# Two graph layers on one core: output shifts, the second group's point at infinity, the first group's distances and masks, the first load's semaphore and the tail's norms in other places of the order

## The chip, the core and the metric

The kernel runs on one core of a Trainium2 chip. The metric is the device time of one execution in microseconds (us); the median of three runs is given. One execution was also recorded by the hardware profiler.

## What is computed

32 graphs of 256 nodes with 128 features pass through two layers with a residual and a layer norm after each:

```python
s = x @ w_se.T + b_se                       # three coordinates per node
A = jnp.exp(-dist(s)) * adj                 # distances, masked
x_nmp = A @ relu(x @ w_msg.T + b_msg)
x_conv = relu(bn2(conv17(relu(bn1(conv1(x))))) + x)
g = gru(input=[x_conv, x_nmp], state=x)     # gates r, z, n
y = layernorm(x + g)
h = (1 + eps) * y + adj @ y
out = layernorm(y + relu(h @ W1 + b1) @ W2 + b2)
```

## The kernel before

Features lie on the 128 partitions. The 32 graphs are worked in eight groups of four (GB = 4), each group as two pairs of graphs with 512 columns (h = 0 and 1). The program is a pipeline written out by hand: each engine has its own list of calls, `prologue`, `steady(s, u, front)` for s = 1 to 7 (s = 3 to 6 in a hardware loop) and `last`. In `steady(s)` the group gb = s - 1 goes through its gates, first norm, aggregation over `adjT`, the two-layer perceptron (`mlp1`, `hidden`, `mlp2`) and second norm, the group gm = s through its messages, distances and convolution, and gf = s + 1 is begun. Nothing but the order of the calls and the semaphore waits in them sets the order of the work.

The 17-tap convolution is worked by interpolation: seven points (HALF, ZERO, PLUS2, MINUS2, PLUS1, MINUS1, INF) have 4 or 5 taps each. A point has a stream of data (`sv`) and a set of weights (`traw`). In groups 0 (all of them), 1 (HALF, ZERO, PLUS2) and 2 (HALF, PLUS2) `plain_taps` multiplies them in float32. Elsewhere `taps` needs each in a high and a low part: ACT makes the high ones (`stream_high` into `sth`, `tap_high` into `wh`), DVE the low ones (`stream_low` into `stl`, `tap_low` into `wl`), and three products stand for one. `W_ORDER` says in which order the weights' parts are made; `w_count(n)` is the count of the semaphores w_high and w_low at which n is ready. The raw weights of ZERO and INF lie in the buffer `tail`, which `hidden` (ACT) and `add_b2` (POOL) write from s = 1 on. The matrices `x`, `nmp`, `xconv` and `h` are split in the same way (`x_low`, `nmp_low`, `xconv_low`, `h_low` on DVE).

What the change touches:

- Start. SP issues `first`, the first pair of x, a part of conv2 and the second pair of x, waits until that pair is there (X_LOADED), and only then issues group 1's x, the identity, the perceptron's weights, group 0's adjacency and the gates' weights. ACT issues three other parts of conv2 and the message weights.
- First group. PE makes the convolution's points with `distances` (four graphs) and `nmp` in between. ACT makes the exponentials (`exps`), POOL masks graphs 0 and 1 (`first_mask`), DVE graphs 2 and 3 (`mask`). DVE adds the points up in `u_sum`, `pair2_sum`, `pair1_sum`, `pair2_add`, `pair1_add`, `inf_add`, and makes group 1's streams (`first_diffs`, `half_stream`, `zero_stream`, `parts2`); POOL's `streams2(1)` follows `parts2(1)`.
- Second group (s = 1, `second_group` on DVE). PE's `taps(1, INF)` wait for `tap_low(INF)` and `stream_low(1, 4)`; behind them stand `mlp1`, `mlp2(0, 0)` and `conv1(2, .)`, and the latter wait for `x_low(2, .)`.
- Every `steady` with front (s = 1 to 6). DVE ends with `nmp_low`, `xconv_low` and `out_shift` of both pairs. `out_shift` (128x4) needs the second norm's 1/deviation from POOL. ACT's `out_norm` (eight activations of 128x128) waits for it; behind `out_norm` ACT has the next stage's `msg_out` and `gates`. PE's fourth gate product (`inn`) uses the bank of the first and so waits for ACT's tanh of it (TR_READY).
- Tail (`last`, group 7). Its second pair is halved: items (0, WHOLE), (1, 0), (1, 1). ACT normalizes the output of the first two, DVE that of the third, each stored by SP in this order.

Of the kernel before, what the change touches and what calls it, by code (L numbers as in the profile page):

```python
# [96 lines left out]
def gnn_kernel(nc, t, out):  # L97
# [10 lines left out]
    with ctx:  # L108
# [99 lines left out]
        W_ORDER = ("conv1", "gates", PLUS1, MINUS2, MINUS1, ZERO, INF, "w1", HALF, PLUS2)  # L208
# [15 lines left out]
        X_LOADED = stage("x_loaded", 16)  # L224
# [84 lines left out]
        x_pair0_loaded = sem("x_pair0_loaded")  # L309
        conv2_loaded = sem("conv2_loaded")  # L310
# [54 lines left out]
        def halved(c):  # L365
            return c in (0, 1)
# [101 lines left out]
        def _(sp):  # L468
# [6 lines left out]
            def store(g, h, c=None):  # L475
                if (h, c) == LAST_ITEMS[-1]:
                    wait(sp, LAST_READY, g, 1)
                else:
                    wait(sp, OT_READY, g, item(h, c) + 1)
# [4 lines left out]
            def prologue():  # L484
# [3 lines left out]
                done(sp.dma_start(xv[0][:, cols(1)], x_v[0, :, cols(1)]), X_LOADED)  # L488
                wait(sp, X_LOADED, 0, 16)
# [34 lines left out]
        def _(pool):  # L524
# [66 lines left out]
            def prologue():  # L591
# [12 lines left out]
                streams2(0)  # L604
                first_mask(0)
# [54 lines left out]
        def _(act):  # L660
# [102 lines left out]
            def prologue():  # L763
# [12 lines left out]
                wait(act, X_LOADED, 0, 16)  # L776
# [26 lines left out]
                tap_high(ZERO)  # L803
# [3 lines left out]
                tap_high(INF)  # L807
                act.wait_ge(mlp_loaded, 16)
                act.activation(w1h[:, :], w1raw, ACT.Copy).then_inc(w_high, 1)
                tap_high(HALF)  # L810
                tap_high(PLUS2)

            def steady(s, u, front):
# [21 lines left out]
                exps(gm, 3)  # L835
                hidden(gb, 0)
# [21 lines left out]
            def last(g, u):  # L858
# [8 lines left out]
                for h, c in LAST_ITEMS[:-1]:  # L867
                    out_norm(g, h, c)
# [5 lines left out]
        def _(dve):  # L874
# [214 lines left out]
            def y_apply(g, h, c=None):  # L1089
                src, v = y_block(h, c), place(h, c)  # L1090
                wait(dve, RSTD[0], g, item(h, c) + 1)
                for q in part_blocks(c):
                    last = dve.tensor_scalar(xn[:, h, q, :], src(q, q + 1), stats[:, 0, v, q, 1:2], rstd[:, 0, v, q:q + 1],  # L1093
                                             ALU.subtract, ALU.mult)
                done(last, XN_READY)
# [43 lines left out]
            def prologue():  # L1139
# [68 lines left out]
                pair2_sum(0)  # L1208
                first_stream1(MINUS1, ALU.subtract)
                taps_step(minus1, minus1, -1.0, even)  # L1210
                mask(0, 0, 3)
                dve.wait_ge(tap_sums, steps[0])
# [3 lines left out]
                parts2(1)  # L1216
                pair1_sum(0)
# [13 lines left out]
            def second_group():  # L1231
# [22 lines left out]
                tap_low(ZERO)  # L1254
                y_apply(0, 1)
                mask(1, 1, 0)
                mask(1, 1, 1)
                inf_stream(1)
                tap_low(INF)
# [3 lines left out]
                h_low(0, 1)  # L1263
                mask(1, 1, 2)
# [4 lines left out]
            def steady(s, u, front):  # L1269
# [40 lines left out]
                if front:  # L1310
# [22 lines left out]
            def last(g, u):  # L1333
# [5 lines left out]
                gates(g, u, 1, 1)  # L1339
# [23 lines left out]
        def _(pe):  # L1363
# [227 lines left out]
            def prologue():  # L1591
# [14 lines left out]
                for b in range(GB):  # L1606
                    distances(0, b)
# [103 lines left out]
```

## Time and profile before

| | us |
|---|---|
| median of 3 runs | 377.34 (377.03 to 377.43) |
| the profiled execution | 380.05 |
| its span (first to last instruction) | 378.2 |
| PE busy | 364.7 (96%) |
| DVE busy | 322.8 (85%) |
| ACT busy | 230.0 (61%) |
| POOL busy | 154.1 (41%) |

PE is the matrix engine (PEld its weight loads), DVE the vector engine, ACT the scalar engine, POOL GpSimd, SP the engine that issues most transfers. In the profile "busy" of PE has modelled ends, so two matmuls that follow at once overlap in it. A number in square brackets is the idle time of the engine before the row, with what released it. L876 is line 876 of the kernel before.

### The profile page before, as it was taken

Reading aid. Unit: us, or ns where it says so; the run is one execution under the profiler, and the core shown is the slowest. Engines: PE = TensorE matmul, PEld = TensorE weight load, DVE = VectorE, ACT = ScalarE, POOL = GpSimd, SP = SyncE. Lnnn points to the kernel's source line nnn. Section 1 sums busy time; section 2 is a strip of 40 time slices with the busy share of each in tenths; the row PEclk is TensorE's granted clock in tenths of the full one; section 3 lists DMA queues with packets and bytes.
Section 4 is the critical chain, followed back from the end, with each engine's and each line's share of the span. In section 5 each row is a group of like instructions: output and inputs, shape, how many; then the busy total and the mean of one; then the engine's idle time right before and its main releaser. Section 6 shows DMA issues by size and latency. Waiting matters only on the chain.

```text
span 378.2 us, 6430 instructions
## 1 busy us (share of the span) xinstructions
PE 364.7 (96%) x2150; PEld 317.2 (84%) x2150; DVE 322.8 (85%) x706; ACT 230.0 (61%) x436; POOL 154.1 (41%) x158
## 2 busy tenths in 40 slices
PE   6999999899899999999999999999999999999994
PEld 4778889698698988899888997989888997988973
DVE  3999999989799988989799897998889897995584
ACT  3455765444867467573866648774676639564765
POOL 3112326136242743528323462517425372234362
PEclk9899999899999999999999999999999999999999
DMA  6700004300113010120112001120101301000002
GB/s 196 270 1 2 0 3 166 113 1 2 55 56 113 1 57 1 55 113 3 55 55 75 39 10 46 55 111 0 55 0 55 111 2 55 2 0 2 0 30 83
DMA packets 8135, 19.39 MB, mean 51 GB/s; under 512 B 688, under 2 KB 5168, under 8 KB 7088
## 3 DMA queue, kind: packets, MB, share of 16 engines
q1 hardware_dynamic: 7536, 18.17, 13.9%
q10 hardware_dynamic: 576, 0.92, 0.7%
q8 instruction: 13, 0.21, 0.2%
q14 instruction: 10, 0.08, 0.1%
HBM read 14.90 MB, written 4.19 MB: 50 GB/s over the span
## 4 chain that ended last, share of the span: by engine, by line
PE 73%; DVE 13%; ACT 6%; POOL 3%; issue 2%; DMA 2%; SPq 0%; ACTq 0%; DVEq 0%
PE back L1368 24%; PE conv L1368 20%; PE back L1482 6%; PE front L1482 5%; PE back L1578 5%; PE conv L1421 3%; PE front L1454 2%; ACT tail L749 2%; PE front L1474 2%; DMA xv<-in_x_dram 2%; PE back L1534 2%; DVE xcl L1036 1%; DVE xn L1093 1%; ACT tail L756 1%; DVE stl L876 1%
## 5 line engine op out<-in xcount | busy, mean ns | idle before, releaser
L1368 PE MATMUL conv<-sth,wh 128*128 128x256 f32 x207 | 62.2, 301 | 1.7 <-DVE wl L1133 1.7
L1368 PE MATMUL conv<-sth,wl 128*128 128x256 f32 x207 | 59.2, 286 | 0.0
L1368 PE MATMUL conv<-stl,wh 128*128 128x256 f32 x207 | 59.1, 286 | 0.0
L552 POOL TENSOR_TENSOR rstd<-rstd,small 128x4 f32<-128x4 f32 (+1 forms) x34 | 38.5, 1134 | 44.5 <-DVE rstd L1075 43.9
L1368 PEld LDWEIGHTS conv<-sth,wh 128*128 128x128 f32 x207 | 39.2, 189 | 3.0 <-DVE wl L1133 1.8
L1368 PEld LDWEIGHTS conv<-stl,wh 128*128 128x128 f32 x207 | 39.3, 190 | 0.2
L1368 PEld LDWEIGHTS conv<-sth,wl 128*128 128x128 f32 x207 | 39.4, 190 | 0.0
L662 ACT ACTIVATE sth<-sv 128x272 fp32r<-128x272 f32 (+1 forms) x33 | 17.3, 524 | 34.4 <-DVE sv L904 18.5
L557 POOL TENSOR_TENSOR xw<-xw,xv 128x512 f32<-128x512 f32 (+1 forms) x15 | 18.5, 1234 | 46.9 <-ACT xw L732 46.9
L749 ACT ACTIVATE tail<-tail,shift,rstd 128x128 f32<-128x128 f32 x60 | 24.1, 482 | 20.6 <-DVE shift L1128 20.6
L589 POOL TENSOR_TENSOR adjT<-adjT,diag 128x256 f32<-128x256 f32 x32 | 27.9, 902 | 7.0 <-DVE msg L950 3.6
L528 POOL TENSOR_TENSOR av<-h 128x544 f32<-128x544 f32 x6 | 8.6, 1436 | 54.0 <-ACT h L677 54.0
L1482 PE MATMUL front<-amat,msg 128*128 128x256 f32 x128 | 29.1, 379 | 0.0
L1482 PE MATMUL back<-adjT,xn 128*128 128x256 f32 x120 | 28.2, 387 | 0.8 <-DVE xn L1093 0.8
L1578 PEld LDWEIGHTS back<-later_w,tail 128*128 128x128 f32 x224 | 26.3, 192 | 0.7
L756 ACT ACTIVATE tail<-back,first_w 128x512 f32<-128x512 f32 (+1 forms) x30 | 20.4, 683 | 10.3 <-PE back L1368 10.3
L1578 PE MATMUL back<-later_w,tail 128*128 128x128 f32 x224 | 26.5, 275 | 0.0
L1482 PEld LDWEIGHTS front<-amat,msg 128*128 128x128 f32 x128 | 23.8, 190 | 2.9
L1482 PEld LDWEIGHTS back<-adjT,xn 128*128 128x128 f32 x120 | 21.9, 189 | 5.2 <-DVE xn L1093 1.4
L1093 DVE TENSOR_SCALAR xn<-back,stats,rstd 128x128 f32<-128x128 f32 x60 | 20.5, 404 | 2.8 <-POOL rstd L552 2.1
L1050 DVE SCALAR_TENSOR_TENSOR gbuf<-gbuf 128x512 f32<-128x512 f32 (+1 forms) x17 | 13.6, 800 | 9.1 <-ACT gbuf L723 9.1
L876 DVE TENSOR_TENSOR stl<-sv,sth 128x272 fp32r<-128x272 f32 (+1 forms) x33 | 18.4, 557 | 3.0 <-ACT sth L662 2.9
(243 smaller groups left out, 1029.2 us busy)
## 6 DMA issues: line engine op xcount, KB each, us to landing
adjT<-in_adj_dram SPq DMA_DIRECT2D x8, 1024.0 KB, 4.8
out_dram<-tail SPq DMA_DIRECT2D x15, 256.0 KB, 2.2
xv<-in_x_dram SPq DMA_DIRECT2D x7, 512.0 KB, 3.3
tail<-in_conv_dram ACTq DMA_DIRECT2D x3, 256.0 KB, 4.6
gbuf<-in_gates_dram SPq DMA_DIRECT2D x1, 576.0 KB, 8.6
xv<-in_x_dram SPq DMA_DIRECT2D x2, 256.0 KB, 5.5
tail<-in_conv_dram SPq DMA_DIRECT2D x1, 320.0 KB, 5.3
later_w<-in_later_dram SPq DMA_DIRECT2D x1, 320.0 KB, 5.7
```

The source lines that it names most:

```text
L552: done(pool.tensor_tensor(rstd[:, k, v, q], rstd[:, k, v, q], minus_half[:, q], ALU.pow), RSTD[k])
L557: done(pool.tensor_tensor(xw[:, h, part(c)], xw[:, h, part(c)], xv[u][:, part_cols(h, c)], ALU.mult), XWX_READY)
L589: done(pool.tensor_tensor(dg, dg, diag[:, :].unsqueeze(1).to_broadcast([P, PAR, P]), ALU.add), ADJE_READY)
L662: done(act.activation(dst, src, ACT.Copy), name)
L749: last = act.activation(o[:, q, :], o[:, q, :], ACT.Identity, bias=shift[:, v, q:q + 1], scale=rstd[:, 1, v, q:q + 1])
L756: done(act.activation(hid[:, h, f, part(c)], bank("hid", h, c, f), ACT.Relu, bias=vec[:, B1 + f:B1 + f + 1]), HID_READY)
L876: done(dve.tensor_tensor(dst, src, full(hi), ALU.subtract), name)
L1050: done(dve.scalar_tensor_tensor(ghn[:, h, part(c)], tr[:, h, part(c)], 1.0, ghn[:, h, part(c)], ALU.add, ALU.mult), T1_READY)
L1093: last = dve.tensor_scalar(xn[:, h, q, :], src(q, q + 1), stats[:, 0, v, q, 1:2], rstd[:, 0, v, q:q + 1], ALU.subtract, ALU.mult)
L1368: ins = pe.matmul(bank, a, b, start=first and k == 0, stop=last and k == len(todo) - 1)
L1482: ins = pe.matmul(tile[:, k * N:(k + 1) * N], lhs(b, rm), rhs(b, rm), start=rm == 0, stop=rm == PAR - 1)
L1578: ins = pe.matmul(tile[:, k * P:(k + 1) * P], hid[:, h, f, q * P:(q + 1) * P], w2[:, f, :], start=f == 0, stop=f == 1)
```

## The change

Calls change places; few waits come or go, and the arithmetic is the same.

- SP issues its first transfers without the wait. The second pair of x has a semaphore of its own, x_pair1_loaded, and X_LOADED counts from group 1.
- First group: PE's distances stand between the taps of MINUS2. DVE's `mask(0, 0, 3)` and `pair2_sum(0)` come behind `parts2(1)`. POOL's masks wait for the weight sum of PLUS1 (tap_sums 10).
- Second group: INF's weights are split before ZERO's, `inf_stream(1)` stands ahead of the masks, `tap_low(ZERO)` behind `h_low(0, 1)`. `hidden` on ACT waits for ZERO's low weights in s = 1. POOL's `add_b2` had that wait and keeps it, but its count is now 8 in place of 6.
- Stages with front: `out_shift(gb, 0)` stands ahead of `nmp_low`, `out_shift(gb, 1)` ahead of `xconv_low`.
- Tail: DVE's first norm of pair 0 is cut in two around `add_input(1, 1)`; PE's aggregation of pair 0 is in one piece behind the last transposes; the output norm of item (1, 0) goes from ACT (two activations and a shift) to DVE (two `tensor_scalar`).

`plain_taps` gets a range of taps, `y_apply` a list of blocks; PE's waits in `plain_conv1` and `messages` follow the new semaphores. The core of the diff:

```diff
-        W_ORDER = ("conv1", "gates", PLUS1, MINUS2, MINUS1, ZERO, INF, "w1", HALF, PLUS2)
+        W_ORDER = ("conv1", "gates", PLUS1, MINUS2, MINUS1, INF, "w1", ZERO, HALF, PLUS2)
...
-        X_LOADED = stage("x_loaded", 16)
+        X_LOADED = stage("x_loaded", 16, 1)
...
             def store(g, h, c=None):
-                if (h, c) == LAST_ITEMS[-1]:
-                    wait(sp, LAST_READY, g, 1)
+                if halved(c):
+                    wait(sp, LAST_READY, g, item(h, c))
...
-                done(sp.dma_start(xv[0][:, cols(1)], x_v[0, :, cols(1)]), X_LOADED)
-                wait(sp, X_LOADED, 0, 16)
+                sp.dma_start(xv[0][:, cols(1)], x_v[0, :, cols(1)]).then_inc(x_pair1_loaded, 16)
                 load_x(1, 1)
...
                 streams2(0)
+                pool.wait_ge(tap_sums, 10)
                 first_mask(0)
...
                 xconv_high(0, 0)
-                tap_high(ZERO)
+                tap_high(INF)
                 nmp_high(0, 1)
                 xconv_high(0, 1)
                 stream_high(1, 2)
-                tap_high(INF)
                 act.wait_ge(mlp_loaded, 16)
                 act.activation(w1h[:, :], w1raw, ACT.Copy).then_inc(w_high, 1)
+                tap_high(ZERO)
...
                 exps(gm, 3)
+                if first:
+                    act.wait_ge(w_low, w_count(ZERO))
                 hidden(gb, 0)
...
-                for h, c in LAST_ITEMS[:-1]:
-                    out_norm(g, h, c)
+                out_norm(g, 0, WHOLE)
...
                 mask(0, 0, 2)
-                pair2_sum(0)
                 first_stream1(MINUS1, ALU.subtract)
                 taps_step(minus1, minus1, -1.0, even)
-                mask(0, 0, 3)
-                dve.wait_ge(tap_sums, steps[0])
                 first_diffs(1)
                 half_stream(1)
                 zero_stream(1)
                 parts2(1)
+                dve.wait_ge(tap_sums, steps[0])
+                mask(0, 0, 3)
+                pair2_sum(0)
                 pair1_sum(0)
...
                 pair2_sum(1)
-                tap_low(ZERO)
+                tap_low(INF)
                 y_apply(0, 1)
+                inf_stream(1)
                 mask(1, 1, 0)
                 mask(1, 1, 1)
-                inf_stream(1)
-                tap_low(INF)
                 stream_low(1, 4)
                 h_low(0, 0)
                 w_low_part(w1l[:, :], w1raw, w1h[:, :], w_count("w1"))
                 h_low(0, 1)
+                tap_low(ZERO)
...
                     stream_low(gf, 2)
+                    out_shift(gb, 0)
                     nmp_low(gm, 0)
                     nmp_low(gm, 1)
+                    out_shift(gb, 1)
                     xconv_low(gm, 0)
                     xconv_low(gm, 1)
-                    out_shift(gb, 0)
-                    out_shift(gb, 1)
...
-                gates(g, u, 1, 1)
-                y_apply(g, 0, WHOLE)
+                reset(g, 1, 1)
+                y_apply(g, 0, WHOLE, (0, 1))
+                add_input(g, 1, 1)
+                y_apply(g, 0, WHOLE, (2, 3))
                 gates_end(g, 1, 1)
...
                 out_stats(g, 1, 1)
-                out_shift(g, 1, 0)
+                out_apply(g, 1, 0)
                 out_apply(g, 1, 1)
...
-                plain_taps(0, MINUS2)
-                for b in range(GB):
-                    distances(0, b)
+                plain_taps(0, MINUS2, 0, 3)
+                distances(0, 0)
+                distances(0, 1)
+                plain_taps(0, MINUS2, 3)
+                distances(0, 2)
+                distances(0, 3)
                 plain_taps(0, PLUS1)
...
                 mlp2(g - 1, 1)
-                aggregate(g, u, 0, WHOLE, (0,))
                 y_transpose(g, 1, 1)
-                aggregate(g, u, 0, WHOLE, (1,))
+                aggregate(g, u, 0, WHOLE)
```

How DVE's order moves in the first group, between `mask(0, 0, 2)` and `pair2_add`; the first sv is MINUS1's stream, amat a mask, av to wv are group 1's streams, pm the sums of point pairs. Before:

```order
L1005 SCALAR_TENSOR_TENSOR pm<-conv,first_w,pm 128x4x64 [waits conv_minus2_ready]
L1005 SCALAR_TENSOR_TENSOR pm<-conv,first_w,pm 128x4x64
L898 TENSOR_TENSOR sv<-vv 128x272 [waits pair1_parts_ready]
L1177 SCALAR_TENSOR_TENSOR adjT<-adjT 128x640 [waits tap_sums]
L982 TENSOR_TENSOR amat<-front,adjT 128x512 [waits adj_loaded,exp_ready]
L891 TENSOR_TENSOR av<-h 128x4x2x68 [waits inf_stream_ready,h1_ready,tap_sums]
L893 TENSOR_TENSOR av<-h 128x4x2x68
L904 SCALAR_TENSOR_TENSOR sv<-av 128x544 [waits sub0_full,token_diffs_ready]
L912 SCALAR_TENSOR_TENSOR sv<-sv 128x272 [waits sub1_full,half_stream_ready]
L917 SCALAR_TENSOR_TENSOR wv<-av 128x272 [waits pair2_streams_ready]
L919 SCALAR_TENSOR_TENSOR wv<-av 128x272
L1018 SCALAR_TENSOR_TENSOR pm<-conv,first_w,pm 128x512 [waits conv_minus1_ready]
```

With the change:

```order
L900 TENSOR_TENSOR sv<-vv 128x272 [waits pair1_parts_ready]
L1180 SCALAR_TENSOR_TENSOR adjT<-adjT 128x640 [waits tap_sums]
L893 TENSOR_TENSOR av<-h 128x4x2x68 [waits inf_stream_ready,h1_ready]
L895 TENSOR_TENSOR av<-h 128x4x2x68
L906 SCALAR_TENSOR_TENSOR sv<-av 128x544 [waits sub0_full,token_diffs_ready]
L914 SCALAR_TENSOR_TENSOR sv<-sv 128x272 [waits sub1_full,half_stream_ready]
L919 SCALAR_TENSOR_TENSOR wv<-av 128x272 [waits pair2_streams_ready]
L921 SCALAR_TENSOR_TENSOR wv<-av 128x272
L984 TENSOR_TENSOR amat<-front,adjT 128x512 [waits adj_loaded,exp_ready,tap_sums]
L1007 SCALAR_TENSOR_TENSOR pm<-conv,first_w,pm 128x4x64 [waits conv_minus2_ready]
L1007 SCALAR_TENSOR_TENSOR pm<-conv,first_w,pm 128x4x64
L1020 SCALAR_TENSOR_TENSOR pm<-conv,first_w,pm 128x512 [waits conv_minus1_ready]
```

The mask of graph 3 and the two `pair2_sum` operations moved behind group 1's streams, next to `pair1_sum`.

DVE in the second group, behind the first norm of pair 1. wl<-tail is a `tap_low`, sv the stream at infinity, stl its low part, nmpl<-back an `h_low`. Before:

```order
L982 TENSOR_TENSOR amat<-front,adjT 128x512 [waits nmp_full,adj_loaded,exp_ready] x2
L938 SCALAR_TENSOR_TENSOR sv<-av 128x4x67 [waits inf_stream_ready]
L942 SCALAR_TENSOR_TENSOR sv<-sv 128x272 [waits sub6_full,inf_part_ready]
L1133 TENSOR_TENSOR wl<-tail,wh 128x512 [waits w_high]
L876 TENSOR_TENSOR stl<-sv,sth 128x272 [waits streams_high_ready]
L876 TENSOR_TENSOR nmpl<-back,nmph 128x512 [waits h_high_ready]
L1133 TENSOR_TENSOR w1l<-later_w,w1h 128x256 [waits w_high]
L876 TENSOR_TENSOR nmpl<-back,nmph 128x512 [waits h_high_ready]
```

With the change:

```order
L940 SCALAR_TENSOR_TENSOR sv<-av 128x4x67 [waits inf_stream_ready]
L944 SCALAR_TENSOR_TENSOR sv<-sv 128x272 [waits sub6_full,inf_part_ready]
L984 TENSOR_TENSOR amat<-front,adjT 128x512 [waits nmp_full,adj_loaded,exp_ready] x2
L878 TENSOR_TENSOR stl<-sv,sth 128x272 [waits streams_high_ready]
L878 TENSOR_TENSOR nmpl<-back,nmph 128x512 [waits h_high_ready]
L1136 TENSOR_TENSOR w1l<-later_w,w1h 128x256 [waits w_high]
L878 TENSOR_TENSOR nmpl<-back,nmph 128x512 [waits h_high_ready]
L1136 TENSOR_TENSOR wl<-tail,wh 128x512 [waits w_high]
```

The stream at infinity moved ahead of the masks, and the `tap_low` that stands here is now ZERO's and comes last.

DVE at the end of a stage with front (s = 1 here; the same in all six). Before:

```order
L876 TENSOR_TENSOR stl<-sv,sth 128x544 [waits streams_high_ready]
L876 TENSOR_TENSOR nmpl<-front,nmph 128x512 [waits nmp_high_ready] x2
L1036 SCALAR_TENSOR_TENSOR xcl<-usum,xch 128x4x128 [waits xconv_high_ready] x2
L1128 SCALAR_TENSOR_TENSOR shift<-stats,rstd 128x4 [waits rstd2_ready] x2
```

With the change:

```order
L878 TENSOR_TENSOR stl<-sv,sth 128x544 [waits streams_high_ready]
L1131 SCALAR_TENSOR_TENSOR shift<-stats,rstd 128x4 [waits rstd2_ready]
L878 TENSOR_TENSOR nmpl<-front,nmph 128x512 [waits nmp_high_ready] x2
L1131 SCALAR_TENSOR_TENSOR shift<-stats,rstd 128x4 [waits rstd2_ready]
L1038 SCALAR_TENSOR_TENSOR xcl<-usum,xch 128x4x128 [waits xconv_high_ready] x2
```

Each shift moved ahead: one before the two `nmp_low`, one before the two `xconv_low`.

## Rows read from the trace of the kernel before

**Rows 1.** Busy time by windows, 60 to 70 us: PE, PEld, DVE, ACT, POOL, granted clock, DMA.
```profile
60.00:70.00 10.00, 8.34 (x54) 6.84 (x53) 9.90 (x22) 4.45 (x10) 6.67 (x6) 1.00 0.31 115
```
**Rows 2.** Timeline of PE, rows with idle time: start, length, engine, line, operation, [idle, releaser].
```profile
69.60 0.36 PE L1368 MATMUL conv<-sth,wh 128*128 128x256 f32 x1 [1.66 <-DVE wl L1133]
97.54 0.50 PE L1368 MATMUL back<-nmph,wh 128*128 128x512 f32 x1 [1.07 <-ACT gbuf L723]
141.93 0.51 PE L1368 MATMUL back<-nmph,wh 128*128 128x512 f32 x1 [0.25 <-ACT gbuf L723]
363.90 1.97 PE L1482 MATMUL back<-adjT,xn 128*128 128x256 f32 x8 [0.76 <-DVE xn L1093]
```
**Rows 3.** The start: PE's row, the second x pair's landing (L488), a window's traffic.
```profile
8.78 1.86 PE L1438 MATMUL conv<-xv,first_w 128*128 128x512 f32 x2 [1.99 <-DMA xv<-in_x_dram]
...
DMA to landing us min/median/max: 6.6/6.6/6.6
...
5.00:6.00 1.00, 1.00 (x4) 0.49 (x3) 0.72 (x6) 0.42 (x1) 0.00 (x0) 1.00 0.95 350
```
**Rows 4.** Timeline of the first group, and one DVE addition of the second.
```profile
26.64 0.99 PE L1474 MATMUL front<-factT 32*128 32x256 f32 x4 [0.68 <-ACT amat L707]
34.98 0.75 DVE L1018 SCALAR_TENSOR_TENSOR pm<-conv,first_w,pm 128x512 f32<-128x512 f32 x1 [0.16 <-ACT pm L697]
35.63 0.76 POOL L538 TENSOR_TENSOR sv<-wv 128x272 f32<-128x272 f32 x1
35.65 1.29 DVE L1013 TENSOR_TENSOR usum<-usum,pm 128x512 f32<-128x512 f32 x1
...
76.08 0.68 DVE L1013 TENSOR_TENSOR usum<-usum,pm 128x512 f32<-128x512 f32 x1
```
**Rows 5.** Timeline of the second group, 65 to 78 us, POOL, DVE and PE.
```profile
65.27 2.50 POOL L567 TENSOR_TENSOR tail<-xn,later_w 128x512 f32<-128x512 f32 x2
66.57 1.49 DVE L938 SCALAR_TENSOR_TENSOR sv<-av 128x268 f32<-128x268 f32 x1
68.10 0.44 DVE L942 SCALAR_TENSOR_TENSOR sv<-sv 128x272 f32<-128x272 f32 x1
74.88 1.28 DVE L876 TENSOR_TENSOR xl<-xv,xh 128x512 fp32r<-128x512 f32 x2
77.12 0.48 PE L1368 MATMUL conv<-xh,wh 128*128 128x512 f32 x1
```
**Rows 6.** The chain that ended last: the same twelve matmuls of `mlp1`, second group and later.
```profile
71.83 3.76 PE back L1368 x12
...
250.34 2.76 PE back L1368 x12
```
**Rows 7.** End of stage 1, timeline and all shifts' durations (ns min/median/max).
```profile
88.30 1.28 DVE L876 TENSOR_TENSOR nmpl<-front,nmph 128x512 fp32r<-128x512 f32 x2
89.63 1.51 PE L1454 MATMUL front<-later_w,xv 128*128 128x132 f32 x12
92.00 3.20 ACT L749 ACTIVATE tail<-tail,shift,rstd 128x128 f32<-128x128 f32 x8 [3.38 <-DVE shift L1128]
...
L1128 DVE SCALAR_TENSOR_TENSOR shift<-stats,rstd x16: 149/164/692, 91.3 to 374.0; 128x4 f32<-128x4 f32 x15, 128x2 f32<-128x2 f32 x1
```
**Rows 8.** The chain that ended last: a pair's 27 gate matmuls, pair 0 and pair 1.
```profile
180.91 6.44 PE back L1368 x27
187.79 6.25 PE back L1368 x27
```
**Rows 9.** Timeline of the tail: ACT's tanh, DVE's product after it, the last stores.
```profile
359.76 0.49 ACT L735 ACTIVATE gbuf<-gbuf,small 128x256 f32<-128x256 f32 x1
360.77 0.41 DVE L1061 TENSOR_TENSOR gbuf<-gbuf 128x256 f32<-128x256 f32 x1
374.68 0.86 ACT L749 ACTIVATE msg<-msg,shift,rstd 128x128 f32<-128x128 f32 x2
375.57 0.84 SPq L482 DMA_DIRECT2D out_dram<-msg  x2
```

More of the change, by code:

```diff
@@ L309, in gnn_kernel @@
         x_pair0_loaded = sem("x_pair0_loaded")
+        x_pair1_loaded = sem("x_pair1_loaded")
         conv2_loaded = sem("conv2_loaded")
@@ L775, in prologue @@
                 h1_out(0, 1)
-                wait(act, X_LOADED, 0, 16)
+                act.wait_ge(x_pair1_loaded, 16)
                 high(xh[0][:, cols(1)], xv[0][:, cols(1)], XH_READY)
@@ L1087, in y_stats, with y_apply @@
                 norm_stats(0, g, h, c, y_block(h, c))
-            def y_apply(g, h, c=None):
+            def y_apply(g, h, c=None, qs=None):
                 src, v = y_block(h, c), place(h, c)
                 wait(dve, RSTD[0], g, item(h, c) + 1)
-                for q in part_blocks(c):
+                for q in part_blocks(c) if qs is None else qs:
                     last = dve.tensor_scalar(xn[:, h, q, :], src(q, q + 1), stats[:, 0, v, q, 1:2], rstd[:, 0, v, q:q + 1],
                                              ALU.subtract, ALU.mult)
-                done(last, XN_READY)
+                if q == part_blocks(c)[-1]:
+                    done(last, XN_READY)
             def h_low(g, h, c=None):
@@ L1394, in taps, with plain_taps @@
                     done(ins, CONV_FULL[n])
-            def plain_taps(g, n):
-                if n == ZERO:
+            def plain_taps(g, n, k0=0, k1=None):
+                k1 = NTAP[n] if k1 is None else k1
+                if k0 > 0:
+                    pass
+                elif n == ZERO:
                     wait(pe, Z_READY, g, 1)
@@ L1418, in plain_taps @@
                 out = inf_out(g) if n == INF else conv_out(n)
-                for k in range(NTAP[n]):
+                for k in range(k0, k1):
                     at = k + 1 if n == ZERO else k
@@ L1422, in plain_taps @@
                                     stop=k == NTAP[n] - 1)
-                done(ins, CONV_FULL[n])
+                if k1 == NTAP[n]:
+                    done(ins, CONV_FULL[n])
             def conv1(g, u, h, ahead=False):
@@ L1435, in plain_conv1 @@
                     pe.wait_ge(x_pair0_loaded, 16)
+                elif g == 0:
+                    pe.wait_ge(x_pair1_loaded, 16)
                 else:
@@ L1440, in messages @@
             def messages(g, u):
-                if isinstance(g, int) and g < 2:
+                if opening(g):
+                    pe.wait_ge(x_pair0_loaded, 16)
+                    pe.wait_ge(x_pair1_loaded, 16)
+                elif isinstance(g, int) and g == 1:
                     wait(pe, X_LOADED, g, 16)
```

## The prediction, made before the changed kernel was run

> **What bounds the kernel now.** I read the busy times by windows first, then PE's timeline for rows with idle time, then the chain that ended last, and around each idle row the timeline of the engine that it names. The reader should see three regimes.
>
> In the first 75 us DVE has no free time: 9.90 of the 10 us from 60 to 70, while PE has 8.34 [rows 1]. What DVE does there is the path, and whatever shortens it moves everything behind it. Between stages PE waits for ACT once per stage: 1.07 us at 97.54, 0.25 us at 141.93 [rows 2]. In the loop no idle time is shown any more, but the 27 gate matmuls of pair 0 take 6.44 us and those of pair 1 take 6.25 us [rows 8]: 0.19 us of waiting and restarting hide in it. In the tail the chain alternates between engines, with 0.76 us of PE waiting for DVE [rows 2], and ends with two stores one behind the other [rows 9]. The largest single idle time of PE is 1.66 us, up to 69.60, for INF's low weights [rows 2]. It costs more than itself: the same twelve matmuls take 3.76 us from 71.83, right after it, and 2.76 us at 250.34 [rows 6].
>
> **The change part by part.** The sum is made against the profiled execution, 380.05 us with a span of 378.2. The median of the runs is 377.34, and I take the difference over unchanged.
>
> *First transfers.* SP no longer waits before it issues group 1's x and what follows. Nothing on the path waits for any of these, so I take no gain. The loss is bounded by what they may take from the transfers before them, since PE idles for the second x pair until 8.78 and the whole start hangs on it [rows 3]. Between zero (a queue serves in order) and an equal share for group 1's x, 0.5 MB at the 350 GB/s of the window [rows 3], that is 1.5 us. I take zero: ahead of the second pair SP already has three transfers queued without a wait, and it landed 6.6 us after its issue [rows 3], which is what 1.8 MB at about that rate (5.2 us) and a landing need. The Trainium skill ("DMA: Bandwidth & Descriptors", section on queues, rings and completion order) says that a completion's semaphore write lands only after every earlier write of that DMA engine, across its queues. By that rule ACT's last conv2 part and message weights could be reported late, behind writes of group 1's x; no row here shows it, and the sum would stay the same unless conv2's delay exceeded that of the x pair.
>
> *First group.* Two paths meet at `pair1_sum`: DVE waits only 0.16 us there for ACT's output of MINUS1, which waits for PE [rows 4]. Both must be relieved for a gain. PE: with two taps of MINUS2 between the distances, the 0.68 us that PE waited for an exponential [rows 4] is filled. DVE: its work up to `pair1_sum` is the same, but `parts2(1)` is done earlier, by a mask and two sums that now follow it, over 1 us of work. So POOL's `streams2(1)`, whose last operation ran from 35.63 to 36.39, is over before DVE's first addition of two SBUF tensors. That addition started at 35.65 and took 1.29 us; the same one without POOL at work takes 0.68 [rows 4]. The gain is 0.61 + 0.16 = 0.77, at least 0 and at most that; I take 0.75, since mask and sums read PSUM and the longer addition is the one operation in this stretch that shows POOL's neighbourhood. POOL's new wait for tap_sums 10 is satisfied when its first exponential is there or soon after (POOL had been idle before), and PE's `nmp` behind it has the 0.68 us in hand.
>
> *Second group.* DVE's work from the masks to `x_low(2, 0)` is only permuted, but POOL's `add_b2` (two, 2.50 us from 65.27) now waits for ZERO's low weights and leaves the stream at infinity alone: 1.49 us beside it against 0.44 for the next one, of the same size [rows 5]. So `x_low(2, 0)` starts at 74.88 - 1.05 = 73.83 and its first half ends some 0.66 later, at 74.5; PE's `conv1(2, 0)` may start at 74.55 in place of 77.12 [rows 5]. On PE the path up to it is free of the 1.66 and of the slow 1.00 [rows 2, 6]: 77.12 - 2.66 = 74.46. The two meet within 0.1 us; the later one decides, **2.57 us**. Behind this stand ACT's h1, POOL's differences and the next stage, all waiting for `conv1(2, .)`, so it carries on. What could be late next: ACT's `hidden` waits for ZERO's low weights, which DVE makes before the last two masks, some 4 us before `x_low`; `h_low(0, 0)` needs ACT, which was idle up to the stream's high part. `add_b2` is wanted only after `mlp2` and may lie anywhere in the 3 us after. The bounds are 1.05 (DVE's alone, if PE finds another wait) and 2.66.
>
> *Shifts, six stages.* `out_norm` starts 3.38 us before the place it has now at the most [rows 7], and the stall it causes is 1.07 + 0.19, 0.25 + 0.19, and 0.19 in each of the four stages behind: 1.26 + 0.44 + 0.76 = 2.46 us [rows 2, 8]. All fit into 3.38. After that ACT waits for `msg_out` on DVE, whose place does not move. The price is on DVE: two shifts ahead of what PE waits for. A shift alone takes 0.16, beside POOL up to 0.69 [rows 7], and POOL adds the diagonals at just this place. In stage 1 the first `nmp_low` ends at about 88.95 and PE's `messages` take it at 89.63 [rows 7]: 0.68 us of cover against 0.69. I subtract 0.1; in later stages three products per tap stand for one ahead of `messages`, and the cover is longer. That is **2.35 us**, with bounds of 0 (the tanh stays as late, held by DVE's messages) and 2.5. The Trainium skill ("SBUF — State Buffer", on the shared port pair) says that DVE with two SBUF inputs and POOL exclude each other for a whole instruction. The trace agrees, with 0.69 against 0.16; by that rule each of the two shifts could wait for one diagonal operation, and the sum would be the same up to the 0.1 already taken.
>
> *Tail.* The product behind ACT's last tanh could start at 360.25 and started at 360.77, behind four blocks of norm [rows 9]; with two of them ahead it starts 0.5 earlier, and the chain up to `aggregate(1, 0)`, where PE idles 0.76 [rows 2], takes 0.48 of that. PE's aggregation of pair 0 ends later, but before that point. At the end ACT's norm of item (1, 0) ended at 375.54 and its store came at 375.57, the last one 0.42 behind it [rows 9]. On DVE it is ready 0.9 earlier, and the last store then goes when item (1, 1) is ready, some 0.35 sooner. Together 0.83, bounds 0.3 and 0.9.
>
> **Sum:** 0.75 + 2.57 + 2.35 + 0.83 = 6.5 us. Profiled 380.05 - 6.5 = 373.55; median 377.34 - 6.5 = **370.8 us**.
>
> **Rivals.**
> - *Transfers crowd the start.* For: the wait removed is one that keeps 2.5 MB away from the x pair. Against: see above. 1.5 us of the gain go, 372.3.
> - *The second group finds another wait*, such as ACT's `h_high` or `hidden` behind ZERO's weights, so that PE stands still as before. For: DVE is full, and ACT's order has a new wait. Against: each input is ready 0.3 us or more before it is needed by the sums above. Only DVE's 1.05 stays, 372.4.
> - *The shifts give nothing*: ACT's tanh is then bound by `messages` on DVE, which the shifts beside POOL push back. 377.34 - 4.15 = 373.2.
> - *Slower than before.* One mechanism: the queue shares its rate among all it holds, so that the second x pair lands behind all five transfers now queued after it, 2.5 MB. At 350 GB/s that is 7.1 us, at the rate that the second pair's own landing shows (1.8 MB in 6.6 us) [rows 3] 9.2 us; with the latter 377.34 - 6.5 + 9.2 = 380.0. It decides from a landing 6.5 us later. Against: such a share would also have spread the three transfers that already stand together.
> - *It does not do what it says* (the norms and shifts are not earlier because they wait for POOL): in the third rival.
>
> **How the numbers follow.** Forecast 0.70, with its own range 369.9 to 371.8 (all terms near their upper bounds; half a microsecond to one lost). Transfers 0.10, second group 0.09, shifts 0.07, share among all 0.03 (of it 0.01 so near the limit that it reads as no change), the first two rivals together 0.01 (373.9). The range from 369.6 to 372.7 takes in the first three cases and leaves out about 0.11. A measurement can tell about 0.2% (0.75 us) from no change. Faster 0.97, same 0.01, slower 0.02.
>
> **What would show it.** In the changed kernel's profile PE should have no idle row of over 0.6 us between 10 and 360 us; INF's first product should follow the distances at once, with the granted clock at 1.00 from 65 to 75 us; DVE's addition in `pair2_add` of group 0 should take 0.68; pair 0's gates should take 6.25 us in the loop, and its inner stage period should fall by 0.2. The last two stores should be issued 0.4 apart with the last right behind DVE. The second x pair should still start PE at about 8.8. I am wrong if PE starts there later, if `conv1(2, 0)` comes later than about 73.8 (74.55 less the first group's 0.75), or if PE waits for the low parts of `nmp` or `xconv` at a stage's beginning.

## The result, and the profile after

The changed kernel took 372.89 us (median of 6 executions, 372.3 to 374.02), the kernel before, run beside it, 377.38 us (377.03 to 378.57). The ratio is 0.9883 (0.9861 to 0.9904): 4.5 us faster, where 6.5 were forecast, and 0.2 us above the range. The profiled executions tell another size: 380.05 us before and 373.07 us after, 6.98 us apart. Nearly every step that I read from the profile holds when profile is compared with profile. What failed lies between the profile and the median.

PE's timeline of the changed kernel (start, length, engine, line, operation, count, in brackets the idle time before the row and what ended it), its rows with idle time, and last the row that had 0.76 us of it in the tail:

```profile
8.97 1.12 PE L1449 MATMUL conv<-xv,first_w 128*128 128x512 f32 x2 [1.66 <-DMA xv<-in_x_dram]
19.50 2.41 PE L1429 MATMUL conv<-sv,first_w 128*128 128x256 f32 x10 [0.20 <-DVE first_w L1180]
26.07 2.41 PE L1429 MATMUL conv<-sv,gbuf 128*128 128x256 f32 x10 [0.32 <-DVE gbuf L1180]
28.75 1.97 PE L1496 MATMUL front<-amat,msg 128*128 128x256 f32 x8 [0.28 <-DVE amat L984]
73.11 0.47 PE L1373 MATMUL conv<-xh,wh 128*128 128x512 f32 x1 [0.26 <-DVE xl L878]
...
354.95 0.41 PE L1548 MATMUL front<-ident_w,gbuf 128*128 128x128 f32 x2 [0.27 <-DVE gbuf L1066]
...
356.99 1.97 PE L1496 MATMUL back<-adjT,xn 128*128 128x256 f32 x8
```

Of the four idle times in [rows 2], 1.66, 1.07, 0.25 and 0.76 us, none is left. In the first group 0.32 and 0.28 us have come in place of the 0.68 of [rows 4], and 0.27 us is new in the tail. New is also 0.26 us ahead of `conv1(2, 0)`: PE now waits there for DVE's `x_low(2, 0)`. The row of 8.97 answers to the first of [rows 3]: the same two matmuls take 1.12 us where they took 1.86.

DVE's and POOL's timeline of the changed kernel, first group and then second (as [rows 4, 5]):

```profile
33.70 0.77 POOL L538 TENSOR_TENSOR sv<-wv 128x272 f32<-128x272 f32 x1
...
34.86 0.68 DVE L1015 TENSOR_TENSOR usum<-usum,pm 128x512 f32<-128x512 f32 x1
...
63.96 0.43 DVE L940 SCALAR_TENSOR_TENSOR sv<-av 128x268 f32<-128x268 f32 x1
...
72.27 1.29 DVE L878 TENSOR_TENSOR xl<-xv,xh 128x512 fp32r<-128x512 f32 x2
...
68.62 2.57 POOL L567 TENSOR_TENSOR tail<-xn,later_w 128x512 f32<-128x512 f32 x2 [4.73 <-DVE wl L1136]
```

POOL's last operation of `streams2(1)` is over at 34.47, before the addition, which takes 0.68 us in place of 1.29. DVE's step of the INF tile takes 0.43 us in place of 1.49, with POOL's `add_b2` 4.7 us behind it.

The chain that ended last, changed kernel (start, length, engine, tile, line, count), answers to [rows 6, 8]:

```profile
94.48 6.25 PE back L1373 x27
...
113.26 2.76 PE back L1373 x12
...
305.95 6.25 PE back L1373 x27
...
312.64 6.25 PE back L1373 x27
```

Pair 0's gates take 6.25 us like pair 1's. The row at 312.64 stood at 319.07 before, so 6.43 us have been gained by then, and the tail adds 0.57 to make 7.0 us of span.

One row more divides the 6.43: the second group's distances, the last PE row ahead of its aggregation, before and after.

```profile
63.18 0.50 PE L1474 MATMUL front<-factT 32*128 32x256 f32 x4
...
61.76 0.50 PE L1488 MATMUL front<-factT 32*128 32x256 f32 x4
```

Up to there 1.42 us are gained, where the sum has 0.75. From there to `conv1(2, 0)` (77.12 to 73.11, 4.01 in all) it is 2.59, where the sum has 2.57, and from there to the row at 312.64 another 2.42, where it has 2.35. The first figure is too large because the profile before holds a stretch of half clock at 9 us that the sum left out, as the next section shows.

### The profile page after: what moved, and what is told of

The parts are those of the page before. It is cut to its first block, busy times and chain, and to the rows that moved or that the text cites. A ratio compares the mean times of both kernels' runs of the same rounds, so it can differ in the third digit from the quotient of the medians.

```text
span 371.2 us, 6429 instructions
## 1 busy us (share of the span) xinstructions
PE 361.3 (97%) x2150; PEld 315.3 (85%) x2150; DVE 319.2 (86%) x707; ACT 232.2 (63%) x434; POOL 153.6 (41%) x158
## 4 chain that ended last, share of the span: by engine, by line
PE 83%; DVE 11%; DMA 2%; issue 1%; ACT 1%; POOL 0%; SPq 0%; POOLq 0%; DVEq 0%
PE back L1373 28%; PE conv L1373 22%; PE front L1496 8%; PE back L1496 6%; PE back L1592 6%; PE conv L1429 3%; PE front L1468 3%; DMA xv<-in_x_dram 2%; PE back L1548 2%; PE front L1488 1%; DVE adjT L1180 1%; PE conv L1468 1%; DVE amat L984 1%; DVE usum L997 1%; DVE xn L1095 1%
## 5 line engine op out<-in xcount | busy, mean ns | idle before, releaser
L589 POOL TENSOR_TENSOR adjT<-adjT,diag 128x256 f32<-128x256 f32 x32 | 25.1, 813 | 7.5 <-DVE usum L1033 3.9
L729 ACT ACTIVATE gbuf<-back,small 128x512 f32<-128x512 f32 x15 | 10.3, 690 | 20.4 <-PE back L1373 20.4
L567 POOL TENSOR_TENSOR tail<-xn,later_w 128x512 f32<-128x512 f32 x15 | 19.9, 1328 | 7.0 <-DVE wl L1136 4.7
```

Of the source, the lines that this page charges most:

```text
L567: done(pool.tensor_tensor(out_tile(h, c)[:, q, :], xn[:, h, q, :], b2bc.unsqueeze(1).to_broadcast([P, len(part_blocks(c)), D]), ALU.add), ...
L589: done(pool.tensor_tensor(dg, dg, diag[:, :].unsqueeze(1).to_broadcast([P, PAR, P]), ALU.add), ADJE_READY)
```

## Where the profile and the median part

The windows of 9 to 12.5 and 70 to 73.5 us (stretch and length, busy time and count of PE, PEld, DVE, ACT and POOL, granted clock, DMA share, GB/s), first the kernel before, then the changed one:

```profile
9.00:12.50 3.50, 3.50 (x12) 2.48 (x12) 2.85 (x5) 1.79 (x4) 0.00 (x0) 0.51 0.80 259
70.00:73.50 3.50, 3.50 (x16) 3.11 (x15) 3.50 (x9) 1.30 (x3) 0.00 (x0) 0.57 0.46 192
```

```profile
9.00:12.50 3.50, 3.50 (x20) 2.67 (x21) 2.96 (x5) 2.36 (x5) 0.00 (x0) 1.00 1.03 417
70.00:73.50 3.50, 3.24 (x23) 2.87 (x22) 3.50 (x9) 1.78 (x3) 1.19 (x1) 1.00 0.09 33
```

In the profiled execution of before PE ran at 1.2 GHz (granted clock about 0.5) in two stretches. Each came right after PE had stood for 1.7 to 2 us: for the second x pair until 8.78, and for INF's low weights until 69.60 [rows 2, 3]. In the profile after, PE is at 2.4 GHz in both windows. For the first of them this is no gain of the change: PE stood there for 1.66 us before 8.97, much as before, and the clock did not fall in this execution. Of the second stretch I had seen the slow matmuls, and put 1.00 us for them into the sum; the first I had not seen.

The question for the experiments was how much of this the median holds. The times answer it. Of the 77 executions of the kernel before that ran beside the experiments, 33 took 376.99 to 378.30 us, 26 took 378.48 to 379.34, and 18 took 379.60 to 380.74. The profiled execution shown before the change, with both stretches, is of the last kind; the runs that give its median of 377.34 are, by their times, of the first.

Each execution's mean granted clock is known too: mostly about 0.998 in the first kind, 0.994 in the second, 0.990 in the third. It sorts less well, because it also counts a fall of the clock behind PE's last matmuls, where PE has nothing left to do. In the profile of `a_warm` below (mean clock 0.995) the clock is full until about 367.5 us and half from there on, and PE's last matmuls start at 363.54. Nine of the 33 fastest executions have only 0.995, which fits. Below, **clear** is the median over the executions with a mean clock of 0.996 or more, all of which are of the first kind. For the kernel before these are 24 executions, with medians of 377.64, 377.42 and 377.71 us on the three chips. Sorted by time instead, the medians are 377.65, 377.38 and 377.65, so the choice matters little.

## The experiments

**The kernels themselves, again.** `b_again` is the kernel before, `a_again` the changed one.

> The kernel before, unchanged, so that each of its runs shows its span and its granted clock. Theory (clock): the one profiled execution of before, 380.05 us at a mean clock of 0.99, held stretches at half clock that its usual runs do not have; runs near 377.3 us will show a mean clock above 0.99 (0.995 or more), and a run near 380 one of 0.99. A sum made on the profiled execution then counts a gain that the median never had. Rival (overhead): the 2.7 us are the same in every part of the program; then all runs show the same clock of 0.99.

`b_again` took 379.06 us, ratio 1.0 (0.9976 to 1.0024), and its executions fell into the same three kinds (5, 4 and 3 of 12 by their times). They do not all show one clock, so the rival is out. The profiled one, 379.44 us, has only the second stretch; its windows:

```profile
9.00:12.50 3.50, 3.04 (x19) 2.37 (x19) 3.43 (x5) 1.59 (x4) 0.00 (x0) 1.00 0.72 208
70.00:73.50 3.50, 3.50 (x14) 3.08 (x14) 3.50 (x8) 0.95 (x2) 0.00 (x0) 0.60 0.31 131
```

> The changed kernel again, beside before on the same chip. Theory (clock): its executions fall into two sets by their mean clock, 0.996 and above at 372.3 to 373.1 us and 0.994 at about 374; against executions of before at 0.998 or more (377.4 to 378.3) it is 5.0 us faster, against those at 0.99 (379.7 to 380.3) 7 us. Rival: one set, 372.9.

`a_again` took 372.54 us (372.29 to 373.01), beside a median of 378.79 of the kernel before: ratio 0.9852 (0.9829 to 0.9876), 6.25 us. Clear against clear it is 372.60 to 377.42, 4.82 us. The slower set near 374 us that the theory expected did not show in these six. So how large the gain looks depends on how many executions of the kernel before draw a stretch of half clock.

**Part by part.** Five kernels take one part each into the kernel before. Of each diff the core:

```diff
 only_start
+                sp.dma_start(xv[0][:, cols(1)], x_v[0, :, cols(1)]).then_inc(x_pair1_loaded, 16)
-                done(sp.dma_start(xv[0][:, cols(1)], x_v[0, :, cols(1)]), X_LOADED)
-                wait(sp, X_LOADED, 0, 16)
 only_first
+                plain_taps(0, MINUS2, 0, 3)
+                distances(0, 0)
+                distances(0, 1)
+                plain_taps(0, MINUS2, 3)
...
 only_second
+        W_ORDER = ("conv1", "gates", PLUS1, MINUS2, MINUS1, INF, "w1", ZERO, HALF, PLUS2)
...
 only_shift
+                    out_shift(gb, 0)
...
 only_tail
+                y_apply(g, 0, WHOLE, (0, 1))
+                add_input(g, 1, 1)
+                y_apply(g, 0, WHOLE, (2, 3))
```

> The kernel before with only the first transfers changed (no wait on SP, a semaphore of its own for the second x pair). The prediction's sum has 0 for it. Theory (clock): at the median within 0.3 us of before; what it can change is whether PE meets a half-clock stretch behind its wait for the second x pair. Rival (crowded start): 0.5 to 1.5 us slower, the second x pair landing later than 6.6 us after its issue.

> The kernel before with only the second group changed (INF's weights and stream first, ZERO's last). The sum has 2.57 us for it. Theory (clock): the part of it that was a stretch at half clock (1.0 to 1.6 us) was not in the usual runs of before, where DVE's x_low decides; the gain at the median is DVE's 1.05 us. Rival: the stall before INF is in every run and draws the clock down in every run; gain 2.5 us.

> The kernel before with only the output shifts moved ahead in the six stages. The sum has 2.35 us for it. Theory: 2.0 to 2.5 us faster at the median, since none of it hangs on the clock; pair 0's 27 gate matmuls take 6.25 us in place of 6.44. Rival (the port): DVE's shifts beside POOL's diagonals push nmp_low or the messages back, gain under 1 us.

> The kernel before with only the first group changed (distances between MINUS2's taps; graph 3's mask and pair2_sum behind group 1's streams; POOL's masks behind tap_sums 10). The sum has 0.75 us for it. Theory: 0.6 to 0.8 us faster among executions without half-clock stretches; DVE's first addition in pair2_add takes 0.68 us. Rival: the gain is eaten where PE or DVE wait for the masks in the new order; 0 to 0.3 us.

> The kernel before with only the tail changed. The sum has 0.83 us for it. Theory: 0.5 to 0.85 us faster; the spans of before and after between PE's group-7 gates and the end differ by 0.57 us in the two profiled executions. Rival: the tail gives nothing of its own, 0 to 0.2 us.

| kernel | median, us | ratio (95%) | clear, us (count) | against clear before, us | term of the sum |
|---|---|---|---|---|---|
| only_start | 378.02 | 1.0001 (0.9981 to 1.0021) | 377.51 (7) | -0.13 | 0 |
| only_first | 377.49 | 0.9986 (0.9966 to 1.0006) | 376.56 (4) | -0.86 | 0.75 |
| only_second | 376.58 | 0.9949 (0.9931 to 0.9967) | 376.55 (9) | -1.09 | 2.57 |
| only_shift | 376.01 | 0.9937 (0.9913 to 0.9961) | 375.32 (4) | -2.32 | 2.35 |
| only_tail | 378.23 | 0.9981 (0.9959 to 1.0004) | 376.86 (4) | -0.56 | 0.83 |
| a_again | 372.54 | 0.9852 (0.9829 to 0.9876) | 372.60 (4) | -4.82 | 6.5 |

Each clear value is set against the clear value of the kernel before on the same chip. The five clear differences add up to 4.96, the whole is 4.82: the parts are additive, and one term is wrong by more than a few tenths, the second group's. Several medians mislead (that of `only_tail` is of an execution with a stretch), the clear ones, of few executions each, carry some 0.2 us of uncertainty (my estimate from their scatter). For `only_first` and `only_tail` the interval of the ratio takes in 1, so their gains rest on four clear executions each; these all lie at 376.35 to 376.90 us, below the fastest of the 23 executions of the kernel before beside them (377.12).

**Why the second group gives 1.1 and not 2.6.** `only_shift` leaves the second group as it was, and its profiled execution has no stretch of half clock. Its DVE and PE there:

```profile
65.42 1.49 DVE L938 SCALAR_TENSOR_TENSOR sv<-av 128x268 f32<-128x268 f32 x1
73.72 1.29 DVE L876 TENSOR_TENSOR xl<-xv,xh 128x512 fp32r<-128x512 f32 x2
```

```profile
68.44 0.36 PE L1368 MATMUL conv<-sth,wh 128*128 128x256 f32 x1 [1.65 <-DVE wl L1133]
...
74.55 0.47 PE L1368 MATMUL conv<-xh,wh 128*128 128x512 f32 x1
```

PE stands the same 1.65 us ahead of INF, and yet `conv1(2, 0)` starts 0.83 us after `x_low(2, 0)`. In the changed kernel, where PE waits for `x_low`, it is 73.11 - 72.27 = 0.84. So at full clock PE arrived at `conv1(2, 0)` about as its input did, stall and all, and the stall seems to have cost nothing. In the profiled execution of before the distance is 77.12 - 74.88 = 2.24 [rows 5], and 1.4 us of it are PE's stretch of half clock: from INF's first product to `conv1(2, 0)` PE took 7.52 us there, 6.11 in `only_shift`. What is left for the median is DVE's 1.05 us, and that can be tested alone: a wait on POOL keeps `add_b2` away from DVE's step, everything else is the kernel before.

```diff
-                    pool.wait_ge(w_low, w_count(ZERO))
+                    pool.wait_ge(w_low, w_count("w1"))
```

> The kernel before, with one wait of GpSimd's changed: its addition of b2 (1.8 us at 65.3 us) waits for the low parts of w1 instead of those of ZERO, so that it no longer runs beside VectorE's step of the INF tile (1.49 us in the trace of before where its like take 0.43). The order of the points, and TensorE's wait ahead of INF, are the kernel before's. Theory (of the second group's part only this contention is worth anything to the median, 1.05 us): 1.0 us less than the kernel before's cheapest executions (377.4 to about 376.4 us), VectorE's INF step at 0.43 to 0.5 us, conv1(2,0) 1 us earlier. Rival (INF in second place is what gives the 1.1 us that only_second showed): 0 to 0.3 us.

It took 376.94 us, ratio 0.9943 (0.9918 to 0.9967), clear 376.55 (6) against 377.71: -1.16 us, as much as the whole of `only_second`. Its DVE and PE:

```profile
65.89 0.43 DVE L938 SCALAR_TENSOR_TENSOR sv<-av 128x268 f32<-128x268 f32 x1
...
73.12 1.28 DVE L876 TENSOR_TENSOR xl<-xv,xh 128x512 fp32r<-128x512 f32 x2
```

```profile
67.84 0.36 PE L1368 MATMUL conv<-sth,wh 128*128 128x256 f32 x1 [0.59 <-DVE wl L1133]
...
73.95 0.47 PE L1368 MATMUL conv<-xh,wh 128*128 128x512 f32 x1
```

The step takes 0.43 us, PE's stall shrinks by the same 1.06 us to 0.59, and `conv1(2, 0)` again stands 0.83 behind `x_low`. The rival, that INF's place in the order gives the 1.1 us, is out. `only_second` has no stall ahead of INF and `only_addb2` still has 0.59 us of it, and both take 376.55 us: that much of the stall costs nothing. Whether the whole 1.65 us cost nothing was not tried alone; the rows above only speak for it. The order gives what the clear medians don't show: no stall, and no stretch of half clock behind one.

> The changed kernel with its second group undone (the order of the points, of the weights' transfers and of their low parts in the first two groups' items s = 1 as in the kernel before), all else changed. Theory (parts add up): 1.1 us more than the changed kernel in executions without a half-clock stretch, 373.6 us, and TensorE stands again 1.6 us on VectorE ahead of INF near 69 us; some executions have the half-clock stretch behind that and take 1.0 us more. Rival (the other parts have moved VectorE enough ahead that INF's low weights come in time): 372.5 us, as the changed kernel.

`no_second` took 374.83 us (373.56 to 376.45), ratio 0.9894 (0.9863 to 0.9925). Its two clear executions have 373.72, where the theory said 373.6; by their mean clock three of the six have one stretch (375.04) and one has both (376.45). Its stall ahead of INF is back, 1.65 us up to 68.54. So without its second group the changed kernel loses about 1 us in clear executions, of which there are only two, and 2 us in the median.

**Are the stretches caused by PE's stops?** Matmuls on zeros, whose result nothing uses, fill them in the kernel before: four while PE waits for the second x pair (`b_warm_start`), and in `b_warm_both` four more while it waits for INF's low weights.

```diff
                 plain_conv1(0, 0, 0)
+                rouse(4)
                 plain_conv1(0, 0, 1)
...
+                    wait(pe, SD2_READY, gm, 2)
+                    for _ in range(4):
+                        pe.matmul(conv_half(INF), padded[:, 0, :], padded[:, 0:2, :].rearrange("p k o -> p (k o)"),
+                                  start=True, stop=True)
                     pe.wait_ge(w_low, w_count(INF))
```

> The kernel before, with four more of its dummy matmuls on zeros on TensorE's queue between its first two items of conv1, where TensorE otherwise stands for about 2 us on the second x pair; nothing of the results changes. Theory (the half-clock stretch at 9 to 12.6 us of the profiled execution of before follows TensorE's idle time there, and only some executions have it, so that it is in the profile and not in the median): the stretch is in no trace of this kernel, the dearest of the three sets of times that the kernel before shows (377.1 to 377.9, 378.5 to 379.4, 379.6 to 380.3 us) is empty, and the cheapest stays at 377.4. Rival (the stretch comes from something else that the executions differ in, such as the transfers): as many executions over 379.5 us as the kernel before has, about one in four.

> As b_warm_start, and four matmuls on zeros more in the second group, ahead of TensorE's wait for the low parts of INF's weights (into the half of PSUM that INF's own first matmul then starts afresh). Theory: neither half-clock stretch (9 to 12.6 us, 70.4 to 73.8 us) comes in any execution; all of them lie at 377.1 to 377.9 us, and the profiled one with them, against 380.05 us for the profiled one of the kernel before. That is 0 against its cheapest executions and about -1.2 us against its median. Rival (the clock falls for a reason other than TensorE's stop): executions of 378.5 us and more are left, and the median stays within 0.4 us of the kernel before's.

| kernel | median, us (range, count) | ratio (95%) | executions over 379.5 us | over 378.2 us |
|---|---|---|---|---|
| before, beside them | 378.68 (376.99 to 380.74, 25) | | 5 | 16 |
| b_warm_start | 377.76 (377.25 to 379.27, 12) | 0.9981 (0.9963 to 1.0) | 0 | 3 |
| b_warm_both | 377.6 (377.23 to 378.2, 11) | 0.9972 (0.9952 to 0.9992) | 0 | 0 |

The windows of `b_warm_start` and, below them, of `b_warm_both`:

```profile
9.00:12.50 3.50, 3.06 (x19) 2.38 (x20) 3.00 (x4) 1.71 (x4) 0.00 (x0) 1.00 0.71 218
70.00:73.50 3.50, 3.50 (x13) 2.82 (x12) 3.50 (x9) 1.20 (x3) 0.00 (x0) 0.55 0.27 108
```

```profile
9.00:12.50 3.50, 3.19 (x20) 2.45 (x19) 3.01 (x5) 2.21 (x5) 0.00 (x0) 1.00 0.78 234
70.00:73.50 3.50, 3.50 (x21) 2.99 (x20) 3.50 (x8) 2.56 (x4) 0.00 (x0) 1.00 0.14 54
```

With both stops filled no execution is above 378.2 us, where 16 of 25 of the kernel before are. The theory had said 377.9 at most; two are at 378.01 and 378.20, at a mean clock of 0.999. The clear times agree within their uncertainty (377.52 against 377.71), so the filling matmuls save only the half clock. For the first stop alone 0 of 12 against 5 of 25 is a weak count. The rival, another reason for the clock, predicted executions of 378.5 us and more, and is out.

**The filling matmuls on top of the change.** `a_warm` is the changed kernel with `rouse(4)` at the same place.

> The changed kernel with four more matmuls of zeros on PE between the first and the second conv1, so that PE is not idle while it waits for the second x pair. Theory (clock): the idle time at the start is what lets the clock fall in some executions; with it filled no execution shows a mean clock of 0.994, all lie near 372.5, and the median is up to 0.5 us below that of the changed kernel. Rival: the fall has another cause; as many executions at 0.994 as without.

It took 372.98 us (372.55 to 373.15), ratio 0.986 (0.9837 to 0.9884): clear 372.88 against 372.60 of `a_again`. That is no gain. By their times neither of the two had a stretch in its six executions: four of the twelve have a mean clock of 0.995, but they took 372.29 to 373.10 us like the others. Two of the six behind the result did have one, by time and clock (373.95 and 374.02 us, mean clock 0.994, against 372.64 for the four others); whether the filling prevents these can't be told from so few.

## Why the prediction missed, step by step

**The step that failed** is the first of its sum: "I take the difference over unchanged". The sum was made against one profiled execution with PE at 1.2 GHz in two stretches, and 1.5 of its 6.5 us were the end of one of them. The executions that make the median of 377.34 have neither. From profile to profile the sum nearly holds (6.98 measured, 6.5 forecast), but part of that is luck: the first stretch is gone without the change having touched the stop ahead of it. That put some 0.7 us into the difference that the sum did not have, while the tail gave 0.26 less than forecast. Against clear executions it had to be made without those 1.5: 0.75 + 1.05 + 2.35 + 0.83 = 4.98, which gives 372.36. Measured were 372.64 in the clear executions behind the result, and 372.89 with the two others. That 372.64, and the 372.54 of `a_again`, lie inside my range is no merit: its upper end was made of rivals that did not happen. The warning stood in my own numbers: a profiled execution 2.7 us over the median of the runs, and a stretch at half clock in it.

- *First transfers, 0:* right. `only_start` gives 0.13 of a gain, within its uncertainty. More was in flight (417 GB/s against 259 in the window at 9 us), and PE started on the second x pair at 8.97, where I had 8.8 and had called a later start a sign of being wrong. But the profiles with the old order have it anywhere from 8.31 (`only_tail`) to 9.38 us (`only_second`), so 0.2 us tell nothing. The share among transfers did not come, nor the rival that hangs on it. My reason, that nothing on the path waits for these transfers, was not quite so: in the profiles with the old order and no stretch at 9 us PE waits 0.31 to 0.53 us for group 1's x near 12 us (0.46 in `b_again`), and with the new order it doesn't. In the profile that I read, half clock hid this wait. By the 0.13 us it is worth little.
- *First group, 0.75:* right in size, 0.86 measured, and in cause, but not in the operation that showed it. DVE's first addition takes only 0.69 to 0.82 us in the kernels with the old first group whose profiles have no stretch at 9 us. In `only_shift` it takes 0.78 us and the operation behind it 1.25, so that the two are over at 36.40. In `only_first` POOL is done before them, and they are over at 35.64:

```profile
34.37 0.68 DVE L1014 TENSOR_TENSOR usum<-usum,pm 128x512 f32<-128x512 f32 x1
34.96 0.68 DVE L1015 SCALAR_TENSOR_TENSOR usum<-pm,usum 128x512 f32<-128x512 f32 x1
```

- *Second group, 2.57:* the term that was mis-sized, 1.09 measured. Its two paths were both computed, but PE's from a row at half clock. At full clock they were level before the change, DVE's decided, and taking 1.66 us of stall out of PE's gives nothing more than DVE's own gain. My own lower bound, DVE's 1.05 alone, was the value. I had tied it to a rival ("PE finds another wait", 0.09) that did not happen; the real reason was not among the rivals.
- *Shifts, 2.35:* right, 2.32 measured. In the changed kernel DVE's shift is out of the way in stage 1 and ACT's eight norms wait 0.42 us for it in place of 3.38 [rows 7]:

```profile
85.04 3.19 ACT L750 ACTIVATE tail<-tail,shift,rstd 128x128 f32<-128x128 f32 x8 [0.42 <-DVE shift L1131]
```

- *Tail, 0.83:* too high, 0.56 measured. Its first part is right: PE's last aggregation stands at 356.99 against 363.90, 6.91 us earlier, of which 6.43 were there before the tail, so 0.48. Of the 0.35 us at the end the span shows only 0.09. DVE's last norm and the last stores:

```profile
367.28 0.72 POOL L552 TENSOR_TENSOR rstd<-rstd,small 128x2 f32<-128x2 f32 x1 [0.60 <-DVE rstd L1077]
```

```profile
368.04 0.60 DVE L1123 TENSOR_SCALAR msg<-msg,stats,rstd 128x128 f32<-128x128 f32 x2 [0.33 <-POOL rstd L552]
```

```profile
368.32 0.95 SPq L483 DMA_DIRECT2D out_dram<-msg  x2
```

Item (1, 1) still waits for POOL's `rstd`, in the same rhythm as before, and DVE's norm of item (1, 0) now stands ahead of it. The last store was issued at 368.8 against 376.0, 0.3 us sooner beyond the 6.91, so this part came as forecast up to the issue, but the span then ran 2.4 us on, not 2.2. Why it did was not tried.

What the profile was to show came nearly in full: no idle row of PE over 0.6 us between 10 and 360 us, INF's first product right behind the distances, full clock from 65 to 75 us, 0.68 us for the addition, 6.25 us for pair 0's gates. Only the start at 8.97 is later than said. `conv1(2, 0)` came at 73.11, earlier than the 73.8 that I asked for; most of these 0.7 us are the first stretch again (1.42 in place of 0.75). All this was blind to the error, since it compared profiles with profiles.

## What to carry to other kernels

Before a sum is made against a profiled execution, compare its time with the runs and look, window by window, for stretches in which PE's granted clock is half, since they also hide waits and shift which operations collide: what they cost belongs in a sum for the median only in the share of the executions that have them. Where two paths meet, redo both at full clock; a stall in sight on one of them may be level with work on the other, and then its removal gives only what the other gives. A stop of PE can be worth filling, even with matmuls on zeros, because that took away the stretches behind it in the kernel before (none of 11 executions above 378.2 us, 16 of 25 without); in the changed kernel it showed no gain.

## What the runs showed of the chip

The same stop of PE, with the same 1.64 to 1.66 us, was followed by half clock in some executions and not in others: after it the granted clock was 0.57 in the profile of before (0.60 in `b_again`, 0.55 in `b_warm_start`), and 1.00 in `only_start`, `only_first` and `only_shift`, and in `no_second`, where the stall ended at 68.54 (its first row is the stretch behind its wait for the second x pair, at half clock):

```profile
9.00:12.50 3.50, 3.50 (x13) 2.62 (x13) 2.69 (x5) 2.00 (x5) 0.00 (x0) 0.53 1.05 421
67.00:70.00 3.00, 1.46 (x12) 1.49 (x13) 2.94 (x7) 2.37 (x5) 0.00 (x0) 1.00 0.77 270
70.00:73.50 3.50, 3.50 (x21) 2.99 (x20) 3.50 (x9) 2.50 (x4) 0.00 (x0) 1.00 0.18 73
```

Each stretch costs the kernel 1.1 to 1.3 us (medians of 377.65, 378.78 and 380.11 us for the three kinds, taken as none, one and two, on one chip). The Trainium skill ("TensorE: Matmul & The Clock Gate", Part 1) says that the chip judges the engine's activity on a beat that doesn't restart with the kernel, so that one kernel shows different counts of slow matmuls from run to run. The three kinds of executions agree with that. What decides in which execution a stop counts was not tried, and stays open.

That POOL beside DVE makes one DVE step of 0.43 us last 1.49 us, and so costs a kernel of 377 us as much as 1.1 us when it falls on the path, was larger than I would have given it alone. The step started at 66.57 and ended at 68.06, 0.29 us behind the end of POOL's two additions at 67.77 [rows 5]; without POOL beside it the same step took 0.43 us in `only_addb2` and in the changed kernel.
